# Attention loops of a tower kernel: scores one pair ahead, transposes and maximum first, the later steps one pair closer

## The chip, the cores and the metric

The kernel runs on one core of one Trainium2 chip. The metric is device time in microseconds (us) of one execution, as the median of several runs. TensorE (PE) multiplies and transposes, VectorE (DVE), ScalarE (ACT) and GpSimd (POOL) do the elementwise work, SyncE (SP) issues most of the transfers (DMA). Every engine runs its own instructions in the order written and waits on semaphores for the others.

## The reference, cut to what matters

The input is 8 sequences of 256 tokens with 192 features. The tower has four encoder layers with banded attention (12 heads of 16 features; a token sees others within 64 positions), a cross-covariance attention, a mixture of four experts, one full attention with 12 heads, and a mixture of eight experts.

```python
scores = einsum('bhcqd,bhckd->bhcqk', qc, kb) / sqrt(d)      # four layers, banded
probs  = softmax(where(allowed, scores, -1e9), axis=-1)
out    = einsum('bhcqk,bhckd->bhcqd', probs, vb)
...
attn = softmax(einsum('bhqd,bhkd->bhqk', q, k) * SCALE)      # one layer, full
out  = einsum('bhqk,bhkd->bhqd', attn, v)
```

## The kernel before, in words

There are five attention loops: four banded ones (`it` 0 to 3) and a full one (`it` = L). Each goes through 96 pairs. A pair is one head of one sequence with both halves of its 256 queries. There are 24 pairs for each group of two sequences (`PAIRS_G`), so four groups.

A pair p passes through these steps, each of which is a helper in the listing:

- `pe_scores` (L540 for the mask, L542): PE writes the scores into one of three PSUM banks (`BS`), so it waits until pair p - 3 has been exponentiated.
- `dve_max` (L789): the negated maximum of each row.
- `act_exp` (L683): two exponentials, into one of six buffers in SBUF.
- `pe_turn_probs` (L561): PE transposes the probabilities (three blocks in a banded loop, four in the full one) into one of two banks (`BT`).
- `act_hi` (L696) copies them as float16 (the high part, `pth`), and `dve_lo` (L796) subtracts that from the bank and keeps the rest (the low part, `ptl`).
- `pe_values` (L582 to L584): high and low part times the values. Six pairs fill a bank, which `dve_finish` (L814 or L818, L819, L822) empties. `pool_scale` (L1039, L1041) divides by the sums.

The loops `pe_attention`, `act_attention` and `dve_attention` fix by hand, for each step number p, which pairs are served and in which order. Between them lie extra steps from the table `STEPS`: in each group the projections of the next group are made ("chunk", L447 to L451 on PE with L668 on ACT; "tile", a transpose L429 with L650, L762 and L763; "v", L457 to L461 on PE with L782 or L784 on DVE). `pe_step` is called last in a PE step, `dve_step` after the maximum in a DVE step.

POOL splits what a chunk gives into three bfloat16 pieces (L1057 to L1060, `pool_pieces`), splits v (L1138 to L1141, `pool_v`), and splits the weights of the output projection (L1023 to L1027). SP writes the pieces to memory (L1070) and reads them back as qx and kx (L1082), two sequences for each group. The scores of a sequence's first head wait for that read (`qk_in`).

Of the kernel before, what the change touches and what calls it, by code (L numbers as in the profile page):

```python
# [33 lines left out]
NT = B * S // P  # L34
# [10 lines left out]
PAIRS = NG * PAIRS_G  # L45
# [74 lines left out]
def build_tower(nc, a, out, stop=None):  # L120
    ctx = ExitStack()
    with ctx:
# [373 lines left out]
        def where(u):  # L496

            return u // (2 * HEADS), u % 2, u // 2 % HEADS
# [31 lines left out]
        def pe_scores(pe, it, p, banded):  # L530
            b, _, hd = where(2 * p)
            pe.wait_ge(exp_done.sem, exp_done.at(it, 2 * p - 4))
            if b == 0 and hd % 4 == 0:
                pe.wait_ge(first_in[hd // 4].sem, first_in[hd // 4].at(it, 16 * READS))
            elif hd == 0:
                pe.wait_ge(qk_in[b % 3].sem, qk_in[b % 3].at(it, 16 * READS * (b // 3 + (b % 3 > 0))))
            n = D if banded else S
            o = scores_at(p, n)
            if banded:
                nc.tensor.matmul(o, ident_bf, mask[:, 2 * b:2 * b + 2, :], start=True, stop=False)  # L540
            for qt in range(2):
                last = nc.tensor.matmul(o[:, qt, :], qx[0:ROWS, b % 3, hd, qt * P:qt * P + P],  # L542
                                        kx[0:ROWS, b % 3, hd, keys(qt, banded)], start=not banded,
                                        stop=qt == 1 or not banded)
            last.then_inc(s_done.sem, 1)
# [10 lines left out]
        def pe_turn_probs(pe, it, p, banded):  # L556

            pe.wait_ge(lo_ready.sem, lo_ready.at(it, p - 1))
            pe.wait_ge(exp_done.sem, exp_done.at(it, 2 * p + 2))
            for c in range(turns(banded)):  # L560
                last = nc.tensor.transpose(bank[BT[p % 2]][:, c * P:c * P + P], probs_at(p, banded, c * P, P),  # L561
                                           ident[:, :])
            last.then_inc(t_done.sem, 1)
# [32 lines left out]
        def pe_attention(pe, it, banded, w, tile, xx, w_out=None):  # L596

            pe.wait_ge(xx_ready.sem, xx_ready.at(*xx(2 * GT)))
            for p in range(PAIRS + 5):
                if p < PAIRS:  # L600
                    pe_scores(pe, it, p, banded)
                if p >= 5:
                    pe_values(pe, it, p - 5, banded)
                if p == 3:
                    pe.wait_ge(y_read.sem, y_read.at(it, 0))
                if 0 <= p - 3 < PAIRS:
                    pe_turn_probs(pe, it, p - 3, banded)
                pe_step(pe, it, p, banded, w, w_out, tile, xx)

        def pe_out(pe, it, w, c0, g, xt):  # L610
# [81 lines left out]
        def act_hi(act, it, p, banded):  # L692
            act.wait_ge(t_done.sem, t_done.at(it, p + 1))
            act.wait_ge(pv_done.sem, pv_done.at(it, p - 2))
            n = turns(banded) * P
            nc.scalar.activation(pth[:, p % 3, 0:n], bank[BT[p % 2]][:, 0:n], ACT.Copy).then_inc(hi_ready.sem, 1)  # L696
# [7 lines left out]

        def act_attention(act, it, banded, tile):

            for p in range(PAIRS + 3):
                if 0 <= p - 3 < PAIRS:
                    act_hi(act, it, p - 3, banded)
                if p < PAIRS:  # L710
                    act_exp(act, it, 2 * p, banded)
                    act_exp(act, it, 2 * p + 1, banded)
                if step(p, banded):
                    kind, a, b = step(p, banded)
                    if kind == "chunk":
                        act_qk(act, it, a, b, banded)
                    elif kind == "tile":
                        tile(a, True)
                    elif kind == "att":
                        act_split(act, it, turned(1, a), a, True)  # L720
# [71 lines left out]
        def dve_lo(dve, it, p, banded):  # L792
            dve.wait_ge(hi_ready.sem, hi_ready.at(it, p + 1))
            dve.wait_ge(pv_done.sem, pv_done.at(it, p - 1))
            n = turns(banded) * P
            nc.vector.tensor_tensor(ptl[:, p % 2, 0:n], bank[BT[p % 2]][:, 0:n], pth[:, p % 3, 0:n], ALU.subtract)\  # L796
                .then_inc(lo_ready.sem, 1)
# [61 lines left out]
        def dve_attention(dve, ch, it, banded, tile):  # L859

            for p in range(PAIRS + 8):
                if 0 <= p - 4 < PAIRS:
                    dve_lo(dve, it, p - 4, banded)
                if p < PAIRS:
                    dve_max(dve, it, p, banded)
                dve_step(dve, ch, it, p, banded, tile)
                if banded:
                    dve_norm_step(dve, ch, it, p - 6, 0, NG - 1, 1)
                if p >= 11 and (p - 11) % 6 < 2 and (p - 11) // 6 < NT:
                    dve_finish(dve, ch, it, (p - 11) // 6, (p - 11) % 6, banded)  # L870

        def dve_residual(dve, ch, it, half, g, hb_n=None):

# [1362 lines left out]
```

## Time and profile before

| | us |
|---|---|
| median of 3 runs | 1839.52 |
| lowest and highest | 1836.33, 1840.29 |
| the profiled execution's own time | 1839.05 |
| span of its trace | 1837.2 |

| engine | busy us | share of the span |
|---|---|---|
| PE matmul | 1475.5 | 80% |
| DVE | 1241.6 | 68% |
| ACT | 978.1 | 53% |
| POOL | 809.0 | 44% |

The span goes from the first to the last instruction of the profiled execution. The shares are averages over stages which have different limits. The five attention loops lie at about 79 to 227, 328 to 476, 577 to 725, 822 to 969 and 1375 to 1525 us of the span. A bracket at the end of a timeline row gives the idle time of that engine before the instruction and the instruction that released it.

### The profile page before, as it was taken

Reading aid. Unit: us, or ns where it says so; the run is one execution under the profiler, and the core shown is the slowest. Engines: PE = TensorE matmul, PEld = TensorE weight load, DVE = VectorE, ACT = ScalarE, POOL = GpSimd, SP = SyncE. Lnnn points to the kernel's source line nnn. Section 1 sums busy time; section 2 is a strip of 40 time slices with the busy share of each in tenths; the row PEclk is TensorE's granted clock in tenths of the full one; section 3 lists DMA queues with packets and bytes.
Section 4 is the critical chain, followed back from the end, with each engine's and each line's share of the span. In section 5 each row is a group of like instructions: output and inputs, shape, how many; then the busy total and the mean of one; then the engine's idle time right before and its main releaser. Section 6 shows DMA issues by size and latency. Waiting matters only on the chain.

```text
span 1837.2 us, 42512 instructions
## 1 busy us (share of the span) xinstructions
PE 1475.5 (80%) x13098; PEld 1248.7 (68%) x13098; DVE 1241.6 (68%) x3530; ACT 978.1 (53%) x2392; POOL 809.0 (44%) x1177
## 2 busy tenths in 40 slices
PE   0588889789798888989888948849949987679994
PEld 0377678677676776777776827719937765569994
DVE  4698966879775989668896662253368997434444
ACT  0478733688434886338883213225528993135552
POOL 5577323675235773247742320024537521135551
PEclk9899989999899998999998967768969996679997
DMA  3265201734005460026430000036625420157774
GB/s 89 66 148 123 42 1 30 177 80 95 1 1 138 87 144 12 1 47 158 97 76 1 1 14 1 1 147 181 192 85 127 90 62 26 56 178 240 242 247 136
DMA packets 121981, 167.27 MB, mean 91 GB/s; under 512 B 21776, under 2 KB 81232, under 8 KB 121616
## 3 DMA queue, kind: packets, MB, share of 16 engines
q1 hardware_dynamic: 114448, 147.19, 31.6%
q0 software_dynamic: 7296, 17.18, 2.8%
q8 instruction: 117, 1.92, 0.5%
q14 instruction: 120, 0.98, 0.2%
HBM read 128.27 MB, written 36.04 MB: 89 GB/s over the span
## 4 chain that ended last, share of the span: by engine, by line
PE 31%; DVE 12%; issue 5%; ACT 2%; DMA 2%; POOL 2%; SPq 0%; POOLq 0%; DVEq 0%; ACTq 0%
PE bank L1462 7%; DVE neg_max L789 3%; PE bank L1448 2%; PE bank L643 2%; PE bank L1449 1%; PE bank L1452 1%; PE bank L1451 1%; PE bank L1450 1%; DVE xn L909 1%; DVE ptl L796 1%; PE bank L1214 1%; PE bank L561 1%; PE bank L429 1%; PE bank L1435 1%; DVE xx L763 1%
## 5 line engine op out<-in xcount | busy, mean ns | idle before, releaser
L683 ACT ACTIVATE prob<-bank,neg_max 128x192 f32<-128x192 f32 (+1 forms) x960 | 362.0, 433 | 75.9 <-DVE neg_max L789 64.2
L789 DVE TENSOR_REDUCE neg_max<-bank 128x2 f32<-128x384 f32 (+1 forms) x480 | 274.6, 573 | 45.6 <-PE bank L542 42.2
L796 DVE TENSOR_TENSOR ptl<-bank,pth 128x384 f16<-128x384 f32 (+1 forms) x480 | 274.2, 571 | 39.1 <-ACT pth L696 25.0
L561 PE MATMUL bank<-ident,prob 128*128 128x128 f32 x1536 | 270.3, 290 | 0.0
L696 ACT ACTIVATE pth<-bank 128x384 f16<-128x384 f32 (+1 forms) x480 | 249.6, 520 | 35.0 <-PE bank L561 30.2
L650 ACT ACTIVATE xx<-bank 128x256 fp32r<-128x256 f32 x256 | 94.5, 383 | 191.1 <-PE bank L429 187.2
L542 PE MATMUL bank<-kx,qx 96*128 96x192 bf16 (+1 forms) x960 | 167.9, 257 | 1.1 <-DVE xx L763 1.1
L561 PEld LDWEIGHTS bank<-ident,prob 128*128 128x128 f32 x1536 | 164.1, 144 | 0.1
L582 PE MATMUL bank<-v,pth 128*128 128x33 bf16 x1152 | 138.6, 180 | 16.9 <-DVE ptl L796 12.0
L540 PE MATMUL bank<-mask,ident 128*128 128x384 bf16 x384 | 130.5, 340 | 20.7 <-DMA kx<-qk_rows 11.8
L731 ACT ACTIVATE fbuf<-bank,b 128x512 f32<-128x512 f32 x96 | 65.6, 687 | 146.1 <-PE bank L451 146.1
L643 PE MATMUL bank<-w,fbuf 128*128 128x192 f32 x768 | 140.6, 326 | 2.0 <-DVE h L886 2.0
L983 POOL TENSOR_SCALAR rstd<-mv 128x4 f32<-128x4 f32 x52 | 12.5, 240 | 283.8 <-DVE mv L899 277.8
L643 PEld LDWEIGHTS bank<-w,fbuf 128*128 128x128 f32 x768 | 128.5, 189 | 12.2 <-issue 5.2
L584 PE MATMUL bank<-v,ptl 128*128 128x33 bf16 x1152 | 136.6, 178 | 0.0
L583 PE MATMUL bank<-v,pth 128*128 128x16 bf16 x1152 | 132.8, 170 | 0.0
L1385 POOL DMA_INDIRECT y_rows<-vf,mask x68 | 80.4, 1182 | 115.5 <-DVE vf L1539 104.5
L582 PEld LDWEIGHTS bank<-v,pth 128*128 128x128 f16 x1152 | 100.0, 96 | 35.7 <-DVE ptl L796 32.5
L429 PE MATMUL bank<-ident,h 128*128 128x128 f32 x256 | 53.5, 315 | 87.5 <-DVE h L938 46.6
L542 PEld LDWEIGHTS bank<-kx,qx 96*128 96x128 bf16 x960 | 95.1, 101 | 35.6 <-issue 4.7
L1462 PE MATMUL bank<-w,fbuf 128*128 128x192 f32 x552 | 112.8, 328 | 0.0
L429 PE MATMUL bank<-ident,xn 128*128 128x128 f32 x256 | 57.1, 338 | 69.1 <-DVE xx L763 39.4
(293 smaller groups left out, 4515.6 us busy)
## 6 DMA issues: line engine op xcount, KB each, us to landing
xn<-in_e_seg SPq DMA_DIRECT2D x34, 768.0 KB, 6.5
w<-in_e_w SPq DMA_DIRECT2D x23, 576.0 KB, 4.2
qk_rows<-fbuf SPq DMA_DIRECT2D x128, 96.0 KB, 2.3
qx<-qk_rows SPq DMA_DIRECT2D x35, 288.0 KB, 4.0
kx<-qk_rows SPq DMA_DIRECT2D x35, 288.0 KB, 5.8
qk_rows<-w SPq DMA_DIRECT2D x80, 96.0 KB, 2.3
qx<-qk_rows SPq DMA_DIRECT2D x35, 192.0 KB, 4.7
kx<-qk_rows SPq DMA_DIRECT2D x35, 192.0 KB, 5.6
```

Of the source, the lines that this page charges most:

```text
L540: nc.tensor.matmul(o, ident_bf, mask[:, 2 * b:2 * b + 2, :], start=True, stop=False)
L542: last = nc.tensor.matmul(o[:, qt, :], qx[0:ROWS, b % 3, hd, qt * P:qt * P + P], kx[0:ROWS, b % 3, hd, keys(qt, banded)], start=not banded ...
L561: last = nc.tensor.transpose(bank[BT[p % 2]][:, c * P:c * P + P], probs_at(p, banded, c * P, P), ident[:, :])
L582: nc.tensor.matmul(o, pth[:, p % 3, w], v[sums], start=first, stop=False)
L583: nc.tensor.matmul(o[third], pth[:, p % 3, w], v[lows], start=False, stop=False)
L584: return nc.tensor.matmul(o, ptl[:, p % 2, w], v[sums], start=False, stop=stop)
L643: last = nc.tensor.matmul(bank[BY[t]][:, 0:D], fbuf[:, (n - 2) % 4, t * P:t * P + P], w2[:, c, :], start=(c == 0), stop=(c == FC - 1))
L683: nc.scalar.activation(probs_at(p, banded, qt * n, n), scores_at(p, n)[:, qt, :], ACT.Exp, bias=neg_max[:, b % 2, hd, qt:qt + 1], scale=1. ...
L696: nc.scalar.activation(pth[:, p % 3, 0:n], bank[BT[p % 2]][:, 0:n], ACT.Copy).then_inc(hi_ready.sem, 1)
L789: nc.vector.tensor_reduce(neg_max[:, b % 2, hd, :], scores_at(p, D if banded else S), AX.X, ALU.max, negate=True).then_inc(max_ready.sem, 1)
L796: nc.vector.tensor_tensor(ptl[:, p % 2, 0:n], bank[BT[p % 2]][:, 0:n], pth[:, p % 3, 0:n], ALU.subtract)\
L1462: last = nc.tensor.matmul(bank[BY[2 * (G % 2) + s]][:, 0:D], fbuf[:, n % 4, s * P:s * P + P], w2_e[G % 3][:, c, :], start=(c == 0), stop=( ...
```

## The change

On PE the scores run one step ahead: step 0 issues the scores of pairs 0 and 1, and step p those of pair p + 1. The transposes of a pair come at step p - 2 instead of p - 3, and stand before the products, which come at p - 4 instead of p - 5. The extra step of PE keeps its number p. On ACT the high part comes one step earlier relative to the exponentials (p - 2 instead of p - 3), still before them. On DVE the maximum comes first and the low part second, for pair p - 3 instead of p - 4. The finish of a bank comes at step 6f + 10 instead of 6f + 11. The PE and ACT loops end one step sooner. Buffers, waits inside the helpers and arithmetic stay.

```diff
-            for p in range(PAIRS + 5):
-                if p < PAIRS:
-                    pe_scores(pe, it, p, banded)
-                if p >= 5:
-                    pe_values(pe, it, p - 5, banded)
-                if p == 3:
+            for p in range(PAIRS + 4):
+                for ahead in ((0, 1) if p == 0 else (p + 1,)):
+                    if ahead < PAIRS:
+                        pe_scores(pe, it, ahead, banded)
+                if p == 2:
                     pe.wait_ge(y_read.sem, y_read.at(it, 0))
-                if 0 <= p - 3 < PAIRS:
-                    pe_turn_probs(pe, it, p - 3, banded)
+                if 0 <= p - 2 < PAIRS:
+                    pe_turn_probs(pe, it, p - 2, banded)
+                if p >= 4:
+                    pe_values(pe, it, p - 4, banded)
                 pe_step(pe, it, p, banded, w, w_out, tile, xx)
...
-            for p in range(PAIRS + 3):
-                if 0 <= p - 3 < PAIRS:
-                    act_hi(act, it, p - 3, banded)
+            for p in range(PAIRS + 2):
+                if 0 <= p - 2 < PAIRS:
+                    act_hi(act, it, p - 2, banded)
...
             for p in range(PAIRS + 8):
-                if 0 <= p - 4 < PAIRS:
-                    dve_lo(dve, it, p - 4, banded)
                 if p < PAIRS:
                     dve_max(dve, it, p, banded)
+                if 0 <= p - 3 < PAIRS:
+                    dve_lo(dve, it, p - 3, banded)
                 dve_step(dve, ch, it, p, banded, tile)
                 if banded:
                     dve_norm_step(dve, ch, it, p - 6, 0, NG - 1, 1)
-                if p >= 11 and (p - 11) % 6 < 2 and (p - 11) // 6 < NT:
-                    dve_finish(dve, ch, it, (p - 11) // 6, (p - 11) % 6, banded)
+                if p >= 10 and (p - 10) % 6 < 2 and (p - 10) // 6 < NT:
+                    dve_finish(dve, ch, it, (p - 10) // 6, (p - 10) % 6, banded)
```

## Rows read from the trace of the kernel before

**Rows 1.** First part of the page: engine, busy us, share of the span, instructions.

```profile
PE 1475.5 (80%) x13098; PEld 1248.7 (68%) x13098; DVE 1241.6 (68%) x3530; ACT 978.1 (53%) x2392; POOL 809.0 (44%) x1177
```

**Rows 2.** Windows over the five loops: length, busy us by engine, PEclk, DMA share, GB/s.

```profile
78.00:228.00 150.00, 130.08 (x1604) 106.21 (x1605) 131.82 (x339) 119.17 (x331) 91.27 (x144) 0.93 0.48 108
327.00:477.00 150.00, 128.85 (x1602) 105.31 (x1603) 129.60 (x333) 118.91 (x330) 90.31 (x142) 0.95 0.47 104
576.00:726.00 150.00, 129.81 (x1604) 106.30 (x1605) 128.94 (x338) 118.79 (x330) 90.81 (x142) 0.94 0.47 104
821.00:971.00 150.00, 130.82 (x1616) 106.20 (x1614) 133.19 (x353) 119.25 (x332) 93.67 (x147) 0.95 0.47 106
1374.00:1526.00 152.00, 133.20 (x1856) 104.75 (x1855) 137.49 (x276) 134.34 (x310) 78.08 (x135) 0.97 0.41 88
```

**Rows 3.** Waits, 78 to 228 us: total us, times, longest us.

```profile
DVE neg_max L789 <- PE bank L542: 9.8, 10, 2.3
PE bank L540 <- DMA kx<-qk_rows: 3.0, 1, 3.0
```

**Rows 4.** Timeline, plain pairs, 133 to 135 us: start, us, engine, line, operation.

```profile
133.04 0.49 ACT L696 ACTIVATE pth<-bank 128x384 f16<-128x384 f32 x1
133.43 0.73 ACT L683 ACTIVATE prob<-bank,neg_max 128x192 f32<-128x192 f32 x2
...
134.04 0.55 DVE L789 TENSOR_REDUCE neg_max<-bank 128x2 f32<-128x384 f32 x1
...
134.32 0.19 PE L582 MATMUL bank<-prob,pth 128*128 128x66 bf16 x1
...
134.56 0.52 PE L561 MATMUL bank<-ident,prob 128*128 128x128 f32 x3
134.56 0.56 DVE L796 TENSOR_TENSOR ptl<-bank,pth 128x384 f16<-128x384 f32 x1
...
134.93 0.33 PE L540 MATMUL bank<-mask,ident 128*128 128x384 bf16 x1
135.04 0.55 DVE L789 TENSOR_REDUCE neg_max<-bank 128x2 f32<-128x384 f32 x1
```

**Rows 5.** Timeline, first loop: first v of group 1, and kx landing.

```profile
107.68 0.34 DVE L782 TENSOR_TENSOR vf<-bank,row_bv 128x192 f32<-128x192 f32 x1
...
108.27 0.35 POOL L1138 CAST v<-vf 128x192 bf16<-128x192 f32 x1 [1.71 <-PE bank L584]
...
154.21 0.47 PE L540 MATMUL bank<-mask,ident 128*128 128x384 bf16 x1 [2.99 <-DMA kx<-qk_rows]
```

**Rows 6.** The chain that ended last, fourth loop: start us, us, what.

```profile
868.12 2.21 POOL wb_second_lo L1027
...
889.29 7.65 DMA kx<-qk_rows
```

**Rows 7.** Timeline around the chunk of step 24, first loop.

```profile
119.69 0.40 PE L451 MATMUL bank<-xx,wa_second_lo 128*128 128x512 f32 x1
...
120.47 0.56 DVE L789 TENSOR_REDUCE neg_max<-bank 128x2 f32<-128x384 f32 x1 [0.44 <-PE bank L542]
120.51 0.53 PE L561 MATMUL bank<-ident,prob 128*128 128x128 f32 x3
...
121.60 0.56 DVE L796 TENSOR_TENSOR ptl<-bank,pth 128x384 f16<-128x384 f32 x1 [0.57 <-PE bank L584]
```

**Rows 8.** Waits of DVE, 158 to 226 us (first loop behind its kx wait).

```profile
DVE neg_max L789 <- PE bank L542: 1.8, 3, 1.2
DVE ptl L796 <- PE bank L584: 1.7, 3, 0.6
DVE ptl L796 <- ACT pth L696: 1.1, 5, 0.4
```

**Rows 9.** Waits of DVE in the full loop, 1374 to 1526 us.

```profile
DVE ptl L796 <- ACT pth L696: 8.5, 10, 2.3
...
DVE neg_max L789 <- PE bank L542: 3.7, 3, 1.9
```

## The prediction, made before the changed kernel was run

> **What bounds the kernel now.** I read the engine table first. PE is busy for 80% of the span and DVE for 68% [rows 1], but these are averages over stages, so I laid windows over the stages that the change touches. The five attention loops take 752 us of windows together [rows 2]. In them DVE is busy for 131.8, 129.6, 128.9, 133.2 and 137.5 us of 150, 150, 150, 150 and 152, so it is the fullest engine except in the third loop, where PE is ahead of it by 0.9 us. ACT has 119 in a banded loop and 134.3 in the full one, where it stands 3 us behind DVE. DVE's idle time in the five windows is 752 - 661.0 = 91.0 us. That is the most that any reordering can give here, and lead-ins are in it.
>
> Then I asked for the waits. DVE's largest wait in the first loop is for scores, 9.8 us in ten places, and in the middle of the loop PE itself stands 3.0 us on the transfer of kx, once [rows 3]. The timeline shows where that transfer comes from: DVE adds the bias of the first v of group 1 at 107.68, POOL takes it up at 108.27, and kx for pair 48 lands at 154.21 [rows 5]. In between, POOL splits v, the output weights and three chunks, and SP writes and reads the pieces. The chain of work that ended last goes through the same place in the fourth loop, over the splitting of the weights and 7.65 us of the kx transfer [rows 6]. So from step 15 to pair 48 a banded loop goes by POOL and SP, not by the three engines whose order is changed.
>
> For the plain pace I took the timeline where nothing extra is in the way. DVE starts a maximum at 134.04, the low part at 134.56 and the next maximum at 135.04: 1.00 us for a pair [rows 4].
>
> **What the change really reorders.** No instruction is added or removed. Written with q = p + 1, PE's cycle was scores q, products q - 5, transposes q - 3, extra step q. It becomes scores q, transposes q - 3, products q - 5, extra step q - 1. So relative to the scores two things change on PE: transposes and products swap, and the extra step follows one set of scores later. DVE's cycle was max q, extra step q, low q - 3, max q + 1. It becomes max q, low q - 3, extra step q, max q + 1: only the extra step moves, behind one low part. ACT had exp q between high q - 3 and high q - 2, and gets it behind high q - 2.
>
> **Part 1, transposes before products.** In the banded loops the products take 134.56 - 134.32 = 0.24 us of PE in front of the transposes [rows 4]. High and low part wait on the transposes, so where DVE stands in front of a low part that gap shrinks by 0.24. The chunk of step 24 shows it: the chunk's last matmul starts at 119.69, the scores follow, the transposes start only at 120.51, and the low part starts at 121.60 after 0.57 us of idle time [rows 7]. Gaps of this kind ("released by L584") sum to 1.7 us in three places behind the kx wait [rows 8]: 3 x 0.24 = 0.72 us a loop.
>
> **Part 2, high part before the exponential.** The low part waits for a high part that stood behind an exponential (0.73 us [rows 4]) on ACT and no longer does. These gaps ("released by L696") are 1.1 us in five places [rows 8], each 0.4 or less, and I let them go whole. Together a banded loop gains 0.72 + 1.1 = 1.82 us behind pair 48. I use this for all four loops, 7.3 us, since their windows agree within 5 us in every engine [rows 2]. Bounds: 0, if a removed gap comes back at the next maximum, and 1.8 + 1.7 + 1.1 = 4.6 us a loop, if all three kinds go.
>
> In front of pair 48 I count nothing. PE has a kx wait of 3.0 us there, and whatever the engines gain makes it longer. If POOL's chain did not cover this, the gain would be up to DVE's share of the 9.8 us [rows 3].
>
> **Part 3, the full loop.** It has the same waits without POOL's limit: 8.5 us of low parts behind high parts in ten places [rows 9]. ACT has 134.3 of 152 us there [rows 2], so it soon becomes the limit. Bounds 0 and 8.5; I take the middle, 4.3, since DVE and ACT are 3 us apart and one of them must stay full.
>
> **Part 4, the extra step behind a low part.** The v of step 15 comes one low part later on DVE, 135.04 - 134.56 = 0.48 us [rows 4]. What is queued behind it is POOL's chain to kx. So kx lands 0.48 us later relative to the pairs, in four banded loops: 1.9 us lost. At the head of a loop the scores of pair 1 are no longer behind chunk 0, which makes the first steps denser, but chunk 2 still waits for ACT, and pair 4 still follows it; DVE's start-up waits are in the 9.8 us [rows 3]. I take 0 for the head, between 0 and 2.3, the longest of them [rows 3]. Its gain would cancel the 0.48. The finish comes at step 6f + 10 with its products in PE's step 6f + 9, before two low parts, so no new wait arises. The tail is shorter by one step, but DVE is full there and its work stays: 0.
>
> **Part 5, the new ring.** High q - 2 now stands in front of exp q. So exp q - 2 releases scores q + 1 (three banks), behind these PE transposes q - 2, ACT copies it, and only then comes exp q. Two pairs take 0.73 for exp, 134.93 to the next group of PE's work some 0.36 (I take the 0.33 of the mask as its floor), 0.52 for the transposes and 0.49 for the copy: 2.07 to 2.11, with three handoffs of about 0.05 some 2.25 us, 1.13 a pair [rows 4]. DVE needs 1.00 when nothing extra comes, but with its extras 131.82 / 96 = 1.37 a pair over the loop [rows 2]. The ring is faster than DVE's average, so I cost it at nothing; DVE's extras cover it. Without the cover it costs 0.13 a pair.
>
> **The sum.** 7.3 + 4.3 - 1.9 = 9.7 us less. The profiled execution took 1839.05 us, 1.85 more than its span of 1837.2 and 0.47 less than the median of 1839.52. 1839.05 - 9.7 = 1829.4.
>
> The Trainium skill (Perfetto Trace Analysis, Optimization Strategy) says to take the most contended engine of a stage, look for the gaps on it and make what they wait for start sooner. DVE's gaps in rows 8 and 9 are such gaps. Followed to the end the rule promises more than my sum, and is the third rival below.
>
> **Rivals.**
>
> *Nothing moves* (time 1838). The kx wait swallows the first half, in the second half the gaps only change place, since PE behind a chunk needs the same time for the same work whatever its order, and in the full loop ACT is 3 us from being the limit [rows 2]. For it: the critical chain over kx [rows 6]. Against it: the low part's gaps in rows 8 and 9 have a cause that the swap takes away. It gives 1839.05 less at most 3.
>
> *Slower by the ring* (1846). One mechanism: where DVE has no extra step for several pairs, exp q waits for high q - 2, low parts and scores come late, and the pace is 1.13 instead of 1.00. In the second half of a banded loop 48 pairs are not covered by kx. If half of them are plain, 24 x 0.13 = 3.1 us a loop and 12.5 in four, less the 7.3 that still come and with the 1.9 of part 4: 1839.05 + 12.5 - 7.3 + 1.9 = 1846. It decides when the idle time of DVE in front of low parts grows over its 2.8 us in the stretch of rows 8. Against it: 1.37 a pair on average.
>
> *All the gaps go* (1808). By the rule named above, with the terms from rows: 4 x 4.6 [rows 8] + 8.5 + 3.7 [rows 9] = 30.6 us. For it: DVE is the fullest engine. Against it: some gaps are PE's own work for a chunk (five matmuls of 0.40 [rows 7]), which no order shortens.
>
> *The change does not do what it says* is not possible here for the order; that it keeps the same relative order for most steps is counted in the first rival.
>
> **How the numbers follow.** The forecast case, 1822 to 1836, has 0.52. Nothing moves has 0.24, the ring 0.15, all or most of the gaps (below 1822) 0.09. Changes of up to 0.2%, 3.7 us, can hardly be told from none with this kernel: faster means below 1835.8, slower above 1843.2. Faster: 0.50 + 0.09 + 0.03 of the second case = 0.62. Same: 0.20 and 0.02 from the edges of the others, 0.22. Slower: 0.16. The range for eight in ten goes down towards the last case and up into the ring: 1817 to 1845.
>
> **What the profile after would show.** If parts 1 and 2 hold, low parts released by L584 and L696 wait under 1.2 us instead of 2.8 in the second half of a banded loop, and under 4.5 instead of 8.5 in the full one. If the cover of the kx wait holds, PE still waits for kx before pair 48, for 3 us or more, and it lands about 46.5 us behind the first v. If the ring is no limit, ACT's exponentials still wait for the maximum and not for L561. I am wrong if PE no longer waits for kx (then the first half gains too), if the waits for scores grow by what the low parts lose, or if a new wait of high parts for transposes appears in plain pairs.

## The result, and the profile after

The changed kernel took 1816.87 us, the median of 4 runs (1811.8 to 1821.7), and the kernel before 1839.09 in the same series: ratio 0.9887, 95% interval 0.9869 to 0.9906. In a second series of 9 runs it took 1823.5 (ratio 0.9920, 0.9891 to 0.9949). So the gain is 15 to 22 us, where 9.7 were predicted. 1816.9 lies just outside the range of 1817 to 1845; the second series lies inside it, so the range alone decides nothing. What was wrong is in the parts of the sum, below.

The profiled execution took 1821.71 us, with a span of 1819.9. Its engine table answers to [rows 1]; the columns are the same.

```profile
PE 1471.7 (81%) x13098; PEld 1254.9 (69%) x13098; DVE 1227.3 (67%) x3530; ACT 971.0 (53%) x2392; POOL 814.1 (45%) x1177
```

No count changed. DVE reports 14 us less busy time for the same 3530 instructions, and that is the first hint: busy time counts overlapping records once, and DVE's records now overlap more and are 10 us shorter in sum, so some of its busy time was waiting. Windows over the five loops answer to [rows 2]; they begin at each loop's first scores.

```profile
79.00:229.00 150.00, 133.55 (x1623) 111.13 (x1621) 132.43 (x352) 117.97 (x332) 92.92 (x148) 0.92 0.48 108
323.50:473.50 150.00, 130.93 (x1621) 108.93 (x1619) 130.00 (x350) 117.94 (x332) 90.78 (x143) 0.94 0.47 104
568.00:718.00 150.00, 131.88 (x1619) 109.62 (x1619) 128.47 (x341) 117.43 (x331) 90.94 (x143) 0.93 0.46 103
811.00:961.00 150.00, 133.50 (x1621) 112.23 (x1619) 133.17 (x354) 116.55 (x331) 93.48 (x146) 0.91 0.47 105
1365.00:1517.00 152.00, 135.10 (x1861) 110.90 (x1861) 135.85 (x277) 132.24 (x311) 77.43 (x133) 0.96 0.41 87
```

A fixed window of 150 us says little here, because 5 us of the next stage have moved into it (DVE has 352 instructions in the first instead of 339). So I measured the loops themselves in every trace, from the first scores to the last product, and inside them the point where the scores of pair 48 start. Sums over the loops, in us:

```
kernel                    four banded + full loop          to pair 48   behind it    all
                                                           (4 loops)    (4 loops)   loops
before                    147.4 147.7 147.5 146.5 + 149.0    302.4        286.7      738.1
changed                   142.2 142.8 144.3 144.2 + 147.9    296.0        277.6      721.4
changed, second trace     142.7 142.0 141.9 144.3 + 146.6    293.8        277.0      717.5
```

The loops gave 16.7 us in the first trace and 20.6 in the second: 6.4 and 8.6 in front of pair 48, 9.1 and 9.7 behind it, 1.1 and 2.4 in the full loop. Cut finer, at the starts of DVE's maxima, the four banded loops take (sums in us):

```
from              to                            before   changed   changed, second trace
first scores      maximum of pair 15            113.6    108.6    106.6
from there        scores of pair 48             188.9    187.4    187.2
from there        maximum of pair 50             20.5     14.5     14.4
from there        maximum of pair 95            241.7    244.3    244.0
from there        last low part                  20.1     14.3     14.2
from there        end of the last product         4.4      4.4      4.4
```

Behind pair 48 nothing was gained in the long run of pairs from 50 to 95. The gain lies at its two ends: right behind the stop on kx, and in the tail. In this order three DVE operations a loop have moved from the tail to before the maximum of pair 95, so the last four rows have to be read together: 6.0 us behind the stop, 3.2 in what follows.

The waits of DVE from 158 to 226 us answer to [rows 8].

```profile
DVE neg_max L790 <- PE bank L542: 1.3, 2, 0.7
...
DVE ptl L797 <- ACT pth L697: 1.2, 4, 0.4
```

The low part no longer waits for transposes in this stretch (1.7 us before); its wait for the high part is still there (1.1 before). ACT and PE have waits in the same stretch that the kernel before had smaller (2.2 us for the first) or not at all (the second).

```profile
ACT pth L697 <- PE bank L561: 4.6, 12, 0.9
PE bank L561 <- DVE ptl L797: 4.1, 4, 2.0
```

The full loop, from 1365 us on, answers to [rows 9]: no wait went there, 9.2 for 8.5 and 4.5 for 3.7 (7.5 and 5.0 in the second trace).

```profile
DVE ptl L797 <- ACT pth L697: 9.2, 13, 2.0
DVE neg_max L790 <- PE bank L542: 4.5, 5, 1.7
```

The first v and the landing of kx in the first loop answer to [rows 5].

```profile
106.48 0.34 DVE L783 TENSOR_TENSOR vf<-bank,row_bv 128x192 f32<-128x192 f32 x1
...
107.07 0.35 POOL L1139 CAST v<-vf 128x192 bf16<-128x192 f32 x1 [1.71 <-PE bank L584]
...
152.17 0.34 PE L540 MATMUL bank<-mask,ident 128*128 128x384 bf16 x1 [0.15 <-DMA kx<-qk_rows]
```

Against its loop's first scores the v comes at 27.5 us instead of 28.4, the chain takes 152.17 - 106.48 = 45.7 us instead of 46.5, and PE stands 0.15 us on kx before pair 48 instead of 2.99. In the second and third loop that wait is 1.9 and 2.1, in the fourth 0.1. It did not go: most of it moved to an earlier point of POOL's chain, the middle keys (`middle`, a copy that POOL makes of rows of the split v), which the products of pair 36 need. Waits of PE in the first loop up to 160 us, before and after:

```profile
PE bank L582 <- POOL middle L1114: 0.4, 1, 0.4
```

```profile
PE bank L582 <- POOL middle L1115: 2.7, 1, 2.7
```

Over the four loops PE stood 11.9 us on kx before pair 48 and 1.1 on the middle keys; now it stands 4.2 and 10.6, so 14.9 us instead of 13.0. The first v comes 3.1 us sooner in sum and the way from v to pair 48 is 3.3 us shorter; that is the 6.4 of the table.

Behind the stop, the scores of pair 49 no longer stand behind the chunk of step 48. Before and after, 3.64 us and 0.93 us behind the row of pair 48:

```profile
157.85 0.34 PE L540 MATMUL bank<-mask,ident 128*128 128x384 bf16 x1
```

```profile
153.10 0.34 PE L540 MATMUL bank<-mask,ident 128*128 128x384 bf16 x1
```

Whether that is the whole reason for the 6.0 us is not settled, nor which edit brings them: in all traces this stretch (scores of pair 48 to maximum of pair 50) takes 14.2 to 16.4 us in four loops where ACT has its new order, and 18.7 to 22.2 where it has the old one, whatever PE and DVE have.

Last, plain pairs, which answer to [rows 4] (rows of DVE and ACT).

```profile
163.27 0.55 DVE L790 TENSOR_REDUCE neg_max<-bank 128x2 f32<-128x384 f32 x1
...
163.38 0.73 ACT L684 ACTIVATE prob<-bank,neg_max 128x192 f32<-128x192 f32 x2
...
163.74 0.54 DVE L797 TENSOR_TENSOR ptl<-bank,pth 128x384 f16<-128x384 f32 x1
...
163.99 0.49 ACT L697 ACTIVATE pth<-bank 128x384 f16<-128x384 f32 x1
...
164.20 0.54 DVE L790 TENSOR_REDUCE neg_max<-bank 128x2 f32<-128x384 f32 x1
...
164.38 0.73 ACT L684 ACTIVATE prob<-bank,neg_max 128x192 f32<-128x192 f32 x2
```

Here DVE takes 164.20 - 163.27 = 0.93 us for a pair, not the 1.00 of [rows 4], while ACT takes 164.38 - 163.38 = 1.00. Neither trace shows idle time on DVE in such a place. The trace before had this pace too, in the first loop's head, where it could have been read: 87.83 - 86.90 = 0.93.

```profile
86.90 0.55 DVE L789 TENSOR_REDUCE neg_max<-bank 128x2 f32<-128x384 f32 x1
...
87.83 0.55 DVE L789 TENSOR_REDUCE neg_max<-bank 128x2 f32<-128x384 f32 x1
```

### The profile page after: what moved, and what is told of

It is laid out like the page before. It is cut to its first block, busy times and chain, and to the rows that moved or that the text cites. A ratio compares the mean times of both kernels' runs of the same rounds, so it can differ in the third digit from the quotient of the medians.

```text
span 1819.9 us, 42518 instructions
## 1 busy us (share of the span) xinstructions
PE 1471.7 (81%) x13098; PEld 1254.9 (69%) x13098; DVE 1227.3 (67%) x3530; ACT 971.0 (53%) x2392; POOL 814.1 (45%) x1177
## 4 chain that ended last, share of the span: by engine, by line
PE 33%; DVE 11%; issue 4%; POOL 3%; ACT 2%; DMA 2%; SPq 0%; POOLq 0%; DVEq 0%; ACTq 0%
PE bank L1463 7%; PE bank L561 2%; PE bank L1449 2%; PE bank L644 2%; DVE ptl L797 1%; PE bank L1450 1%; DVE neg_max L790 1%; PE bank L1453 1%; PE bank L1452 1%; PE bank L1451 1%; DVE xn L910 1%; PE bank L1215 1%; PE bank L429 1%; PE bank L1436 1%; PE bank L542 1%
## 5 line engine op out<-in xcount | busy, mean ns | idle before, releaser
L684 ACT ACTIVATE prob<-bank,neg_max 128x192 f32<-128x192 f32 (+1 forms) x960 | 369.5, 451 | 21.9 <-DVE neg_max L790 21.3
L561 PE MATMUL bank<-ident,prob 128*128 128x128 f32 x1536 | 265.4, 286 | 43.8 <-DVE ptl L797 33.1
L790 DVE TENSOR_REDUCE neg_max<-bank 128x2 f32<-128x384 f32 (+1 forms) x480 | 270.9, 566 | 36.9 <-PE bank L542 32.9
L561 PEld LDWEIGHTS bank<-ident,prob 128*128 128x128 f32 x1536 | 173.5, 144 | 78.7 <-DVE ptl L797 62.9
L542 PEld LDWEIGHTS bank<-kx,qx 96*128 96x128 bf16 x960 | 89.5, 101 | 39.5 <-ACT prob L684 7.5
L763 DVE TENSOR_TENSOR xx<-bank,xx 128x128 fp32r<-128x128 f32 x256 | 72.7, 284 | 56.9 <-ACT xx L651 56.2
L1505 ACT ACTIVATE fbuf<-bank,b 128x256 f32<-128x256 f32 x138 | 65.5, 475 | 78.5 <-PE bank L1453 77.8
```

Of the source, the lines that this page charges most:

```text
L684: nc.scalar.activation(probs_at(p, banded, qt * n, n), scores_at(p, n)[:, qt, :], ACT.Exp, bias=neg_max[:, b % 2, hd, qt:qt + 1], scale=1. ...
L790: nc.vector.tensor_reduce(neg_max[:, b % 2, hd, :], scores_at(p, D if banded else S), AX.X, ALU.max, negate=True).then_inc(max_ready.sem, 1)
```

## The experiments

All ratios are against the kernel before, run beside it on the same chip. The change has three parts by engine (PE's order, ACT's, DVE's), so I first undid or did them one by one.

**The changed kernel again (a_again), and three parts undone, one in each kernel.**

> The changed kernel once more, unaltered, for a second profile and for the size of the gain with more runs. Theory A (the attention loops carry the gain): the spans from the first score of a banded loop to the first score of the next are again 4.5, 4.1 and 2.6 us shorter than before within 1 us each, and what differs outside the loops (6.0 us in the first profile after the full loop) changes with the profile; ratio 0.987 to 0.992. Rival B (the gain lies outside the loops): the stretch behind the full loop is again 6 us shorter.

Measured 1823.5 us (0.9920, 0.9891 to 0.9949), used above.

```diff
# a_vfirst, in pe_attention
+                if p >= 4:
+                    pe_values(pe, it, p - 4, banded)
                 if p == 2:
                     pe.wait_ge(y_read.sem, y_read.at(it, 0))
                 if 0 <= p - 2 < PAIRS:
                     pe_turn_probs(pe, it, p - 2, banded)
-                if p >= 4:
-                    pe_values(pe, it, p - 4, banded)
# a_act: act_attention as in the kernel before
-            for p in range(PAIRS + 2):
-                if 0 <= p - 2 < PAIRS:
-                    act_hi(act, it, p - 2, banded)
+            for p in range(PAIRS + 3):
+                if 0 <= p - 3 < PAIRS:
+                    act_hi(act, it, p - 3, banded)
# a_dve: dve_attention as in the kernel before
+                if 0 <= p - 4 < PAIRS:
+                    dve_lo(dve, it, p - 4, banded)
                 if p < PAIRS:
                     dve_max(dve, it, p, banded)
-                if 0 <= p - 3 < PAIRS:
-                    dve_lo(dve, it, p - 3, banded)
...
-                if p >= 10 and (p - 10) % 6 < 2 and (p - 10) // 6 < NT:
+                if p >= 11 and (p - 11) % 6 < 2 and (p - 11) // 6 < NT:
```

> The changed kernel with one part undone: the products stand before the transposes on PE again, all else as changed. Theory A (the swap is worth 0.24 us for every low part that DVE waits for): 0.7 us a banded loop and about 2 in the full one lost, 5 us in all, so about 1822. Rival C (with the high part in front of the exponential, transposes are on a ring through all engines, so that the swap is what makes the new order work): 0.24 us in most of 480 pairs lost, 20 to 60 us slower than the changed kernel, slower than before.

> The changed kernel with ACT's order as it was before: the high part comes behind the exponential and the projection copy again, PE and DVE as changed. Theory A (part 2 of the prediction, high part earlier): the 1.1 us a banded loop and 4.3 in the full one are lost, about 9 us, so 1825. Rival D (the high part in front of the exponential costs as much as it gives, since the exponential then waits for the transposes): no difference or up to 10 us faster than the changed kernel.

> The changed kernel with DVE's order as it was before: low part p - 4, maximum p, extra step, finish at 6f + 11; PE and ACT as changed. Theory A: only part 4 goes (v of step 15 one low part earlier: 0.48 us a banded loop for the chain over POOL to kx), about 2 us faster or no difference. Rival E (the extra step behind the low part is what keeps the rest fed: PE gets its transposes' bank back one operation sooner): 4 to 10 us slower than the changed kernel.

Measured: a_vfirst 1824.9 us (0.9928, 0.9911 to 0.9944), a_act 1880.2 (1.0232, 1.0210 to 1.0254), a_dve 1861.2 (1.0130, 1.0111 to 1.0149). By this run the swap of transposes and products is 1 to 8 us of the gain. But taking back either of the two small edits on ACT and DVE does not give back a few us: it costs 38 to 63 and ends well above the kernel before. So I did the reverse.

**The parts done alone in the kernel before.** b_pe, b_act and b_dve take one engine's order from the changed kernel, b_act_dve takes two.

> The kernel before with PE's order alone changed: scores one pair ahead of the extra step, transposes first, products behind. Matched set: ScalarE and DVE ask for nothing sooner, so PE only has more lead; the maximum's wait for scores at the loop heads and behind chunks shrinks, first scores of the chain's v unchanged: 1825 to 1842. If PE's order carries the whole gain by itself: 1817 to 1822. If PE's order also needs the others (because scores q+1 wait for a bank that exponential q-2 frees): 1850 and more, with PE waiting for L683.

> The kernel before with ScalarE's order alone changed: high part q-2 in front of exponential q; PE and DVE keep theirs. Matched set (my theory): PE does the transposes of pair q-2 only in its step q+1, behind the extra step q, so exponential q now waits for work that PE issues a step later. New waits of the high part for transposes (L561) of some 1 us wherever PE has a chunk; 1870 to 1920 us, 30 to 80 slower than before. Additive parts (rival): the low part finds its high part done, 1 us a loop less, 1830 to 1838.

> The kernel before with DVE's order alone changed: maximum, low part q-3 one step sooner, extra step behind it, finish one step sooner. Matched set: low part q-3 asks for transposes and a high part of the same step, which PE issues behind scores and products and ScalarE behind an exponential; 10 to 40 us slower, shown as low parts waiting for the high part (L696) and for transposes (L584), above 5 us in the second half of the first loop. Additive parts: a few us either way, 1832 to 1843.

> The kernel before with ScalarE's and DVE's order changed and PE's old one, products ahead of transposes and the extra step ahead of the transposes of pair q-2. Matched set: as with ScalarE alone, the ring exponential, extra step, scores, transposes, high part closes over every chunk; 1870 to 1920. Additive parts: nearly the changed kernel, 1820 to 1830.

With the runs above, all eight combinations are measured:

```
PE's order   ACT's   DVE's    us        ratio to before (95%)
old          old     old      1838      1          (before)
old          new     old      1926.9    1.0472 (1.0434 to 1.0510)   b_act
old          old     new      1906.1    1.0366 (1.0331 to 1.0402)   b_dve
old          new     new      1943.6    1.0571 (1.0536 to 1.0606)   b_act_dve
new          old     old      1871.2    1.0180 (1.0141 to 1.0219)   b_pe
new          new     old      1861.2    1.0130 (1.0111 to 1.0149)   a_dve
new          old     new      1880.2    1.0232 (1.0210 to 1.0254)   a_act
new          new     new      1816.9    0.9887 (0.9869 to 0.9906)   the change
```

Only the two matched sets, all old and all new, are fast. Alone the parts cost 33, 89 and 68 us; together they gain 22. I had b_pe wrong: I expected about nothing of it. Its waits from 158 to 226 us say where its 33 us go.

```profile
PE bank L561 <- DVE ptl L797: 11.6, 19, 1.4
ACT prob L684 <- DVE neg_max L790: 8.1, 19, 0.9
DVE ptl L797 <- ACT pth L697: 6.2, 5, 1.9
```

And the chunk of step 24 in its timeline, which answers to [rows 7], shows one such place.

```profile
120.16 0.40 PE L451 MATMUL bank<-xx,wa_second_lo 128*128 128x512 f32 x1
...
120.67 0.78 ACT L669 ACTIVATE qf<-bank,bqk,columns 128x512 f32<-128x512 f32 x1 [0.90 <-PE bank L451]
...
121.86 0.56 DVE L797 TENSOR_TENSOR ptl<-bank,pth 128x384 f16<-128x384 f32 x1 [1.93 <-ACT pth L697]
...
122.47 0.55 PE L561 MATMUL bank<-ident,prob 128*128 128x128 f32 x3 [0.68 <-DVE ptl L797]
```

PE now issues the chunk one set of scores and one group of transposes later than ACT's queue expects it. ACT reaches the chunk's eviction 0.90 us too soon and stands on it, with a high part queued behind it whose transposes are long done. DVE waits 1.93 us for that high part, and PE then 0.68 us for the low part. In the changed kernel ACT does that high part first and DVE one more low part. The same chunk, from its timeline:

```profile
118.53 0.40 PE L451 MATMUL bank<-xx,wa_second_lo 128*128 128x512 f32 x1
...
119.04 0.78 ACT L669 ACTIVATE qf<-bank,bqk,columns 128x512 f32<-128x512 f32 x1 [0.46 <-PE bank L451]
...
119.31 0.56 DVE L790 TENSOR_REDUCE neg_max<-bank 128x2 f32<-128x384 f32 x1 [0.55 <-PE bank L542]
...
120.23 0.56 DVE L797 TENSOR_TENSOR ptl<-bank,pth 128x384 f16<-128x384 f32 x1 [0.37 <-ACT pth L697]
```

The other direction, ACT ahead of PE, shows in b_act over the same stretch: the high part stands in front of the exponential and waits for transposes that PE issues behind a chunk.

```profile
ACT pth L696 <- PE bank L561: 12.6, 21, 1.5
```

**The place of PE's extra step alone (a_pestep).** The changed kernel with

```diff
-            for p in range(PAIRS + 4):
-                for ahead in ((0, 1) if p == 0 else (p + 1,)):
-                    if ahead < PAIRS:
-                        pe_scores(pe, it, ahead, banded)
-                if p == 2:
+            for p in range(PAIRS + 5):
+                if p < PAIRS:
+                    pe_scores(pe, it, p, banded)
+                if p == 3:
                     pe.wait_ge(y_read.sem, y_read.at(it, 0))
-                if 0 <= p - 2 < PAIRS:
-                    pe_turn_probs(pe, it, p - 2, banded)
-                if p >= 4:
-                    pe_values(pe, it, p - 4, banded)
+                if 0 <= p - 3 < PAIRS:
+                    pe_turn_probs(pe, it, p - 3, banded)
+                if p >= 5:
+                    pe_values(pe, it, p - 5, banded)
                 pe_step(pe, it, p, banded, w, w_out, tile, xx)
```

> The changed kernel, with PE's extra step back in its old place: scores q, transposes q-3, products q-5, extra step q. Only the place of the extra step against the scores differs from the changed kernel. Matched set (theory): the high part in front of exponential q now waits for transposes behind the extra step, so every chunk stops ScalarE and DVE: 1900 to 1950, with more than 12 us of ScalarE's waits on L561 in the second half of the first loop. Rival, as the prediction had it (the extra step's place costs 0.48 us a loop): 1817 to 1828.

Measured 1891.3 us (1.0271, 1.0241 to 1.0301): 68 to 74 us above the changed kernel, for moving the extra step past one set of scores. The waits from 158 to 226 us name ACT's high part again.

```profile
ACT pth L696 <- PE bank L561: 14.3, 18, 1.2
```

**The loop's head (a_head).** The scores of pair 1 stay behind the first extra step: `for ahead in ((0,) if p == 0 else (1, 2) if p == 1 else (p + 1,))`.

> The changed kernel, but the scores of pair 1 stay behind PE's first extra step, as before the change; from pair 2 on nothing differs. My theory for the first half: the loop's head got denser, so the first v of group 1, and with it POOL's chain to kx and pair 48, come sooner. If so, the first v comes about 1 us later in each banded loop (28.5 instead of 27.5 us behind the first scores) and pair 48 with it: 3 to 8 us slower than the changed kernel, 1823 to 1830. Rival: the head doesn't matter, since DVE catches up before step 15: equal to the changed kernel, 1817 to 1824.

Measured 1818.5 us (0.9880, 0.9836 to 0.9923), so the changed kernel's time. The first v comes at 27.6, 28.2, 28.0 and 29.1 us of the four loops, against 27.5, 27.5, 28.2 and 29.1. My theory for the first half falls: without the denser head the v comes 0.6 us later in the sum of the four loops (2.6 against the second trace), where 1 us in each was expected, and the loops take 720.0 us, between the 721.4 and 717.5 of the changed kernel. The interval leaves room for 8 us either way, so the loops say more here than the time. What brings the v forward must lie behind the head, in the steps up to 15; no run shows which part it is.

**The swap alone (b_swap).** The kernel before with transposes in front of products, scores and extra step where they were.

> The kernel before with PE's transposes in front of its products in each step and nothing else. The prediction's part 1: 0.72 us a banded loop behind pair 48, nothing in front of it, so 1833 to 1838. If transposes in front stop PE on the low part that has to free their bank while the products could have run (as in the run with PE's order alone, which cost 33 us): 1842 to 1870, with PE's waits for the low part at L561. If swap and place of the extra step are separate: within 2 us of before.

Measured 1833.4 us (0.9984, 0.9968 to 1.0000): 3 us, at the edge of what can be told. Part 1 had 0.72 x 4 = 2.9. In its trace the loops are 6.3 us shorter (731.8), of which 3.8 in front of pair 48, where part 1 counted nothing, and 3.3 behind it, while the full loop is 0.8 longer.

**POOL's chain (a_late_w, b_late_w).** POOL splits the output weights between the pieces that lead to kx. Both kernels move that behind the next pieces:

```diff
                 pool_middle(pool, ch, it, 2)
-                pool.wait_ge(rows_y.sem, rows_y.at(it, 16 * 8))
-                alone(pool)
-                pool_weights(ch, wb, SEG).then_inc(wb_ready.sem, 1)
                 pool_pieces(pool, ch, it, 2)
                 pool_middle(pool, ch, it, 3)
+                pool.wait_ge(rows_y.sem, rows_y.at(it, 16 * 8))
+                alone(pool)
+                pool_weights(ch, wb, SEG).then_inc(wb_ready.sem, 1)
                 pool_v(pool, ch, it, 2)
```

> The changed kernel, with POOL's splitting of the output weights moved behind its next pieces and middle keys, so that nothing of the weights stands in POOL's way to kx of pair 48 (some 6 us of POOL). If POOL's chain bounds the first half: kx of pair 48 lands 4 to 7 us sooner, PE's wait of 1.7 us for it in the first loop goes, 1.5 to 2.5 us a banded loop, 1808 to 1816. If DVE, PE and ScalarE bound it and the wait for kx is slack: 1817 to 1824. A cost: the middle keys may come in the way elsewhere, 0 to 5 us.

> The kernel before, with the same move of POOL's weights. The prediction had POOL's chain to kx as what bounds steps 15 to 48 of a banded loop. If so, this alone gives 2 to 3 us a banded loop, 1826 to 1831, pair 48 about 3 us earlier than its 75.2. If the three engines bound it: 1835 to 1840.

Measured: a_late_w 1816.1 us (0.9877, 0.9843 to 0.9912), b_late_w 1832.6 (0.9968, 0.9948 to 0.9988). In a_late_w pair 48 starts at 69.7, 67.8, 69.8 and 67.6 us, 3.7 to 7.1 sooner, so POOL's chain does set the pace up to there. But pair 72 is where it was in the first loop (104.9), and PE has the wait for kx again, now before that pair:

```profile
PE bank L540 <- DMA kx<-qk_rows: 1.7, 1, 1.7
PE bank L582 <- POOL middle L1115: 1.6, 1, 1.6
```

In b_late_w pair 48 starts 2.7 to 4.3 us sooner than in the kernel before, and the time fell by 6 to 7 us, where 8 to 13 were expected. The work was only moved from one delivery into the next. So it has to go behind the last.

**Out of the chain altogether (a_late3, a_late6, b_late6, a_late6v).** In a_late3 the three lines stand behind `pool_middle(..., 5)`, in a_late6 and b_late6 behind the last v, `pool_middle(..., 6)` and `pool_scale(pool, it, NT - 6)`. a_late6v has also a_vfirst's edit.

> The changed kernel with POOL's splitting of the output weights moved further back, behind the pieces of group 3 and the middle keys 5, where POOL should have a gap before the last v. If POOL's chain is what bounds pair 48 and then pair 72: both come 4 to 6 us earlier than in the changed kernel, the waits for kx go, a banded loop is 2 to 4 us shorter, 1803 to 1812. If the three engines bound the loop as a whole and only exchange one wait for another: pair 48 and 72 early, the end where it was, 1814 to 1822.

> As the one before, but the splitting stands behind the last v and middle keys 6, where POOL has idle time already. Same gain if POOL's chain is the bound (1803 to 1812), less what the output projection at the loop's end waits for its weights: about 1 to 3 us a banded loop, so 1806 to 1822. If that wait is long, slower than the changed kernel.

> The kernel before, with POOL's splitting of the output weights behind the last v and middle keys 6. If POOL's chain covered gains of the new order, the two kernels are further apart without it than the 18 to 22 us they are with it: this one 1828 to 1836, so 25 to 33 us above the 1803.3 of the changed kernel with the same move. If the chain covered nothing, and gains by the two edits simply add: 1803.3 + 20 = about 1823. If the old order depended on it more than the new one: below 1820.

> The changed kernel with the weights behind the last v and middle keys 6, and the products in front of the transposes again. In the changed kernel as it stands the swap made 2 to 4 us at most (1824.9 against 1816.9 and 1823.5). If the swap's gain was swallowed by POOL's chain, it shows here: 1808 to 1815. If the swap is worth about nothing in the new order because transposes then stop PE on the low part: 1801 to 1807.

Measured: a_late3 1816.2 us (0.9892, 0.9871 to 0.9912), a_late6 1803.3 (0.9824, 0.9802 to 0.9846), b_late6 1823.7 (0.9934, 0.9911 to 0.9957), a_late6v 1820.3 (0.9907, 0.9887 to 0.9927). In a_late3 pair 72 is early too (101.2 us), but the last v and keys come late, and PE waits for them:

```profile
PE bank L582 <- POOL prob L1115: 2.9, 1, 2.9
```

In a_late6 this wait is gone. What is left there in the first loop is small, the last row being the price of the move:

```profile
PE bank L540 <- DMA kx<-qk_rows: 1.1, 1, 1.1
...
PE bank L457 <- POOL wb_second_lo L1028: 0.6, 1, 0.6
```

a_late6 beats both kernels. The loop table with these (sums as above):

```
kernel      to pair 48   all loops
before         302.4       738.1
b_late6        288.6       723.6
changed        296.0       721.4   (second trace 293.8, 717.5)
a_late6        280.0       707.2
```

Relieving the chain gives the old order 14.5 us and the new one 14.2 (10.3 from the second trace); the new order gives 16.7 to 20.6 with the weights in the chain and 16.4 without. In total the two gains add, within the 4 us by which the two traces differ. In their parts they don't: in the four banded loops the new order gives 15.6 and 18.2 with the weights in the chain and 13.1 without, and the full loop, which this move does not touch, makes up for it with 3.3 instead of 1.1 and 2.4.

For a_late6v I had the wrong answer. The swap, worth about 3 us in the old order and 1 to 8 in the changed kernel, makes 17 us of time here, 13.8 of them in the loops (3.1 in the full loop). Why it is worth more there I have not settled.

## Why the prediction was wrong

**In front of pair 48, the step that failed.** The prediction said "whatever the engines gain makes it longer" of the kx wait, counted nothing there, and took off 1.9 for part 4. Measured: 6.4 us gained (8.6 in the second trace), so 8.3 of the missing us are here. That POOL's chain sets the pace from step 15 to pair 48 was right: a_late_w moved pair 48 by up to 7.1 us, and the chain's length of 46.5 us was 45.7 after. What was wrong is that such a chain is a cover for all of the first half. It begins at a v that the three engines have to reach first, so it is a term of a sum: every us they gain up to that v arrives at pair 48. The two traces of the changed kernel show it: in their eight banded loops the first v comes between 26.4 and 29.1 us, and pair 48 always 45.5 to 46.0 us behind it. This is 3.1 of the 6.4 us, and 5.1 of the 8.6. For what runs beside the chain the prediction was right in kind: PE's waits for POOL there grew by 1.9 us, from 13.0 to 14.9, though most of them now end at the middle keys. b_late6 and a_late6 fit: with the weights out of the chain the new order gives 8.6 us in front of pair 48, not more in sum than the 6.4 and 8.6 with them, but only 1.0 of it by an earlier v and 7.6 beside the chain. The other 0.8 us a loop came off the chain itself, in the first loop all of it behind POOL, in the transfers: from the v to the end of POOL's middle keys it took 36.2 us instead of 35.9. What did that I have not settled.

**Parts 1 and 2, behind pair 48**: 7.3 us predicted, 9.1 and 9.7 measured, and that these are near is luck. The low part's waits [rows 8] fell from 2.8 to 1.2 us, at the edge of "under 1.2", but what went is the wait for transposes. The wait for the high part, which part 2 let go whole, is 1.2 after 1.1, and other waits came: between the maxima of pairs 50 and 95 DVE's recorded idle time in four loops grew from 9.8 to 16.9 us. In the same stretch waiting that was hidden in its durations went (next paragraph). The 6.0 us right behind the stop on kx came from a place that the prediction did not look at, and the tail, "DVE is full there and its work stays: 0", is 5.8 us shorter, 3.2 together with the run of pairs in front of it, which took over some of its work. Part 1 alone measured 3 us for the 2.9 predicted (b_swap), but over half of what its banded loops gained lies in front of pair 48. The working too was of the wrong kind. It priced each edit by the gap that it closes, with the others taken as given. By that rule the edits on ACT and on DVE should each have gained or cost nothing; alone they cost 89 and 68 us.

**DVE's plain pace, in part 5.** "DVE needs 1.00 when nothing extra comes" was read from starts 0.52 and 0.48 us apart with no idle time between them [rows 4]. It needs 0.93, as both traces show. ACT's high part and exponential have 1.00 in both traces, so it looks as if the old order kept DVE in step with ACT, and the wait was hidden inside DVE's durations. Of the 95 distances between maxima in the first loop, 27 are 1.00 to 1.01 us before and none is after. 27 x 0.07 = 1.9 us a loop is the most that this can be, 7.6 in four; it holds some of what parts 1 and 2 were credited with, not more on top. The new ring, put at 1.13 a pair and costed at nothing, does not show as a limit: in the first loop some 30 exponentials start 0.98 to 1.02 us behind those of the pair before, but none sooner, so one plain pair costs ACT 1.0 us and DVE 0.93.

**Part 3, the full loop**: 4.3 predicted, 1.1 and 2.4 measured (147.9 and 146.6 us for 149.0). The waits for high parts were to fall under 4.5 and stayed at 9.2 and 7.5. Five traces have this same full loop (these two, a_late_w, a_late3, a_late6), with 145.6 to 148.4 us, so it gave 0.6 to 3.4. ACT with 132 of 152 us was probably nearer to being the limit than "the middle" allowed; no run tests that.

**Part 4**: the head at 0 was right (a_head). The v of step 15 came 0.9, 1.4 and 1.6 us sooner in three loops and 0.8 later in the fourth; 0.48 later was predicted for all. a_pestep shows what the place of the extra step is really worth: 68 to 74 us when the other two queues are laid out for the other place.

**The signs to look for.** "A new wait of high parts for transposes" was named as a sign of being wrong. It came, and the kernel was faster. ACT's waits in the first loop, before and after:

```profile
ACT prob L683 <- DVE neg_max L789: 14.4, 25, 1.8
ACT pth L696 <- PE bank L561: 7.1, 7, 3.2
```

```profile
ACT pth L697 <- PE bank L561: 13.7, 26, 4.0
...
ACT prob L684 <- DVE neg_max L790: 4.8, 6, 1.5
```

In these rows ACT waits no more than it did, 18.5 us for 21.5, but for another engine. It has time to spare, so only the sum would have told. The other sign, "I am wrong if PE no longer waits for kx (then the first half gains too)", came in part: the wait, forecast at 3 us or more, is 0.1 to 2.1, and the first half did gain. But it was no sign that the chain had stopped setting the pace, since it moved to the middle keys.

**The rivals.** "Nothing moves" rested on the same reading of the kx wait as a cover. "Slower by the ring" (1846) did not come. "All the gaps go" (1808) named 30.6 us; the loops gave 16.7 and 20.6. The Trainium skill (Perfetto Trace Analysis, Optimization Strategy) has one look for the gaps on the fullest engine. Here some of what went was no gap in the trace (the 0.93 against 1.00 above), the gaps between pairs 50 and 95 grew, and in the full loop they stayed.

**Outside the loops**, which the change does not touch, the two profiled executions differ by 0.6 us in all; single stretches move more, as the last section shows. The loops' 16.7 us are the span's 17.3. The median gained 4.9 more than that, and the second series (15) less, so the size of the gain is known to about 4 us either way.

## What to carry to other kernels

When several engines run one software pipeline, the place of an extra step in one queue and the work put in front of it in the others are one choice. Price and test such an order as a whole, since one part of it can cost three to four times what the whole gains. A transfer that is waited for hides gains only of what runs beside its chain; what stands in front of the chain's first instruction is added to it in full. When a wait for such a chain shrinks, look whether it has moved to another thing that the same chain delivers. An engine that shows no idle time but starts the same instructions further apart than elsewhere is probably waiting: compare the distances of starts, not only the idle time. And compare a loop piece by piece: a sum that comes out near the forecast can be made of other parts.

## What the runs showed of the chip

DVE's recorded durations of 0.54 to 0.56 us overlap. Maximum and low part start 0.46 and 0.47 us after one another when nothing holds them, and the 0.52 and 0.48 of [rows 4] are recorded with the same durations and no idle time. So a wait of some 0.05 us does not show.

TensorE's granted clock moves time between stretches that no edit touched. The stretch from the fourth loop to the full loop took 401.7 to 412.3 us in 19 traces, with the same instructions: 401.7 to 405.7 at a granted clock of 0.80, 409.8 to 412.3 at 0.77. Windows over it, of the kernel before, the changed kernel and a_head; the granted clock stands third from the end:

```profile
969.00:1375.30 406.30, 304.69 (x1735) 259.22 (x1734) 196.34 (x685) 133.64 (x292) 115.59 (x149) 0.79 0.22 70
```

```profile
955.10:1365.10 410.00, 308.60 (x1738) 257.18 (x1736) 196.68 (x687) 134.56 (x292) 115.69 (x149) 0.77 0.21 69
```

```profile
956.70:1359.80 403.10, 300.48 (x1735) 255.68 (x1734) 196.68 (x687) 133.82 (x292) 115.59 (x149) 0.80 0.22 70
```

Behind the full loop it is partly given back: 312.9, 306.9 and 313.1 us at 0.84, 0.86 and 0.82. The loops' own lengths differ by 4 us between the two traces of the changed kernel. So with this kernel a change of 5 us in the loops can be read from their own lengths, and not from one execution's total.
